# The last convolution's result moves to its own PSUM bank and runs half a tile later

## The reference

```python
x = x + _L0_conv_ref(_gn(x), ...)  # 25 overlapping patches an image, each convolved by the expert its gate picks
x = x + _L1_conv_ref(_gn(x), ...)  # 3x3 convolution, weights mixed per image by a sigmoid gate
x = x + _L2_conv_ref(_gn(x), ...)  # each pixel replaced by the nearest of 512 codebook vectors
x = x + _L3_conv_ref(_gn(x), ...)  # deformable 3x3: nine bilinear samples a pixel, then a 288 x 32 product
```

## Time and profile before

| | |
|---|---|
| median of 3 runs | 1956.34 us (1949.91 to 1961.21) |
| the profiled execution's own time | 1952.65 us |
| its span, first to last instruction | 1950.4 us |
| busy PE, DVE, POOL, ACT | 1593.0, 1442.8, 1208.6, 1102.4 us |
| mean granted TensorE clock | 0.926 of full speed |
| 280 us to 1786 us: fronts with halves between | seven periods of some 218 to 222 us |
| 1786 us to 1950 us: halves alone | PE busy 158.70 of 164.00 us |

### The profile page before, as it was taken

The page is one execution under the profiler, slowest core; times in us unless marked ns, Lnnn a source line. Parts: engine busy times, 40 slices in busy tenths (PEclk is TensorE's granted clock), DMA queues, the critical chain, the costliest instruction groups (busy, mean ns, idle before and its releaser), DMA issues.

```text
span 1950.4 us, 41631 instructions
## 1 busy us (share of the span) xinstructions
PE 1593.0 (82%) x15426; PEld 1302.8 (67%) x15426; DVE 1442.8 (74%) x2960; ACT 1102.4 (57%) x1499; POOL 1208.6 (62%) x1413
## 2 busy tenths in 40 slices
PE   0239557889988897989888898889988898989998
PEld 0112355669856786668866787658865797668998
DVE  3147546888779877888679778897779767896776
ACT  0001155558655676557655575657755585657986
POOL 4004245777657856677657756677657765677764
PEclk9955578999989999999999999999999998999999
DMA  7954695569846896569856796569856795235542
GB/s 145 212 116 119 148 214 169 150 179 228 219 125 188 206 219 182 150 172 234 219 148 188 185 220 195 151 172 239 220 155 179 188 228 154 76 87 155 150 148 79
DMA packets 294772, 336.84 MB, mean 173 GB/s; under 512 B 219600, under 2 KB 233936, under 8 KB 290348
## 3 DMA queue, kind: packets, MB, share of 16 engines
q1 hardware_dynamic: 240712, 228.88, 45.6%
q0 software_dynamic: 36336, 84.55, 17.8%
q10 hardware_dynamic: 17524, 20.75, 3.6%
HBM read 260.57 MB, written 60.09 MB: 164 GB/s over the span
## 4 chain that ended last, share of the span: by engine, by line
PE 46%; DVE 14%; DMA 11%; DVEq 7%; SPq 6%; issue 6%; ACT 4%; POOL 3%; ACTq 2%
PE bank L1307 25%; PE bank L1406 5%; DMA words<-in_codebook,code 5%; SPq L437 4%; PE bank L1294 4%; DVE code L1183 4%; DVEq L1182 3%; PE bank L1364 3%; PE bank L1391 3%; DVEq L976 3%; PE bank L1276 2%; PE bank L1291 2%; POOL words L622 2%; POOL fetched L599 2%; DVE samp L977 2%
## 5 line engine op out<-in xcount | busy, mean ns | idle before, releaser
L599 POOL DMA_INDIRECT fetched<-row_pairs,corner x768 | 738.8, 962 | 451.5 <-DVE weighted L971 248.7
L1307 PE MATMUL bank<-lent,tent 128*128 128x160 f32 x6144 | 955.3, 310 | 0.4 <-issue 0.4
L1307 PEld LDWEIGHTS bank<-lent,tent 128*128 128x128 f32 x6144 | 881.0, 196 | 95.9 <-issue 68.5
L733 ACT ACTIVATE tent<-lent,row_at_sb 128x768 f32<-128x768 f32 x512 | 449.2, 925 | 54.9 <-PE bank L1307 40.1
L963 DVE TENSOR_TENSOR strip<-bank,near 128x480 f32<-128x480 f32 x512 | 331.9, 651 | 186.0 <-PE bank L1307 181.0
L737 ACT ACTIVATE tent<-tent 128x1536 f32<-128x1536 f32 x256 | 380.0, 1484 | 21.0 <-issue 0.4
L622 POOL DMA_INDIRECT words<-in_codebook,code x256 | 244.0, 953 | 106.2 <-DVE code L1183 54.0
L977 DVE TENSOR_REDUCE samp<-strip 128x96 f32<-128x480 f32 x414 | 270.3, 653 | 39.6 <-issue 2.2
L1406 PE MATMUL bank<-cb,xs 64*128 64x512 f32 x512 | 245.8, 697 | 36.8 <-DVE code L1183 22.1
L819 ACT COPY xs<-xn 32x128 f32<-32x128 f32 x256 | 75.6, 295 | 259.9 <-PE bank L1406 242.5
L722 ACT COPY samp_t<-bank 96x384 f32<-96x384 f32 x256 | 119.9, 468 | 134.7 <-PE bank L1294 111.2
(11 more groups left out here) (136 smaller groups left out, 1113.1 us busy)
## 6 DMA issues: line engine op xcount, KB each, us to landing
lent<-z_rows SPq DMA_DIRECT2D x256, 384.0 KB
picked_weights<-arena SPq DMA_DIRECT2D x14, 1800.0 KB
arena<-picked_weights SPq DMA_DIRECT2D x21, 720.0 KB
arena<-windows SPq DMA_DIRECT2D x288, 50.0 KB
arena<-xp SPq DMA_DIRECT2D x96, 136.0 KB
fetched<-row_pairs,corner POOLq DMA_INDIRECT x768
arena<-row_pairs SPq DMA_DIRECT2D x64, 160.0 KB
slice<-picked_weights SPq DMA_DIRECT2D x14, 720.0 KB
```

Source lines behind the costliest of these rows:

```text
L599: pool.indirect_dma_start(fetched[:, N % FETCHES, k].rearrange("p q c -> p (q c)"), None, pairs_dram[b % 2], bass.IndirectOffsetOnAxis(ap= ...
L733: act.activation(w[:, piece], zs[:, N % SPREADS, :], ACT.Abs, bias=row_at[:, piece:piece + 1])
L1307: m = pe.matmul(STRIPS[j % 3][:, XW * C * e:XW * C * (e + 1)], tent[:, N % TENTS, c, DENSE * d + e], picture[:, b % 2, i, c], start=(c == ...
```

## The change

The result of the last convolution gets the first 128 columns of bank P2, in which nothing else lives any more. The wait of `turn_samples` for `copy_result` goes, and `convolve` waits for the `copy_result` before the last instead. `convolve` moves from half d = 1 of every fourth tile to half d = 0 of the tile after: it now stands in halves -12, -4, 4, 12, 20, 28, 36 and 44, after the strips and before `turn_samples`. `copy_result` moves from the start of half d = 0 to the half d = 1 after it, behind `copy_samples`. DVE's `add_x` and SP's `store` move one tile later. conv1 writes P0 and P1 in place of P1 and P2, and the cells P4 and P1 in place of P2 and P4. As the offsets still stand in P1, PE waits before the second set of cell transposes for the four DVE instructions that read them.

```diff
-        PO = PT[:, 384:512]
+        PO = P2[:, 0:128]
...
-        CELLS = [P2, P4]
+        CELLS = [P4, P1]
...
+        off_read = sem("off_read")
...
-                if n == 5 and b > 0:
+                if n == 6 and b > 0:
                     store(b - 1, 1)
-                if n == 21:
+                if n == 22:
                     store(b, 0)
...
-                if d == 0 and N % SET == 2 and N > SET:
-                    copy_result(N // SET - 1)
                 if d == 1 and N > 1:
                     copy_samples(N - 2)
+                if d == 1 and N % SET == 2 and N > SET:
+                    copy_result(N // SET - 1)
...
-                if n == 3 and d == 1 and b > 0:
+                if n == 4 and d == 1 and b > 0:
                     add_x(b - 1, 1)
-                if n == 19 and d == 1:
+                if n == 20 and d == 1:
                     add_x(b, 0)
...
-                    dve.tensor_tensor(x, x, PP[1 + h][:, :], ALU.add).then_inc(x2_ready, 1)
+                    dve.tensor_tensor(x, x, PP[h][:, :], ALU.add).then_inc(x2_ready, 1)
...
-                        dve.tensor_tensor(dst, src, at_grid.broadcast_to([128, IMG, ht, TAPS]), ALU.add)
+                        dve.tensor_tensor(dst, src, at_grid.broadcast_to([128, IMG, ht, TAPS]), ALU.add).then_inc(off_read, 1)
...
             def convolve(k):
                 pe.wait_ge(samp_sb, SET * (k + 1))
+                if k > 0:
+                    pe.wait_ge(result_sb, k)
...
-                if N >= SET:
-                    pe.wait_ge(result_sb, N // SET)
...
                 strips(N, d)
-                if d == 1 and N % SET == 1 and N > SET:
+                if d == 0 and N % SET == 2 and N > SET:
                     convolve(N // SET - 1)
...
-                            m = pe.matmul(PP[1 + h][C * i:C * (i + 1), :], mix[:, i, C * dx:C * (dx + 1)],
+                            m = pe.matmul(PP[h][C * i:C * (i + 1), :], mix[:, i, C * dx:C * (dx + 1)],
...
                     if f >= 2:
                         pe.wait_ge(cells_sb, FLATS * g + f - 1)
+                    if f == 1:
+                        pe.wait_ge(off_read, 4 * (g + 1))
```

## The result

The changed kernel takes 1940.71 us (median of 11 runs, 1931.53 to 1957.64), the kernel before 1956.34 in the same comparison. The ratio is 0.9917, 95% interval 0.9893 to 0.994: faster by 0.8%, some 16 us, where 42 were forecast. It lies above the range of 1893 to 1938. The profiled span is 1934.9 us after 1950.4.

What follows compares the result with a forecast made beforehand. PE was taken as busiest yet idle some 357 us, with 84.4 us of waits touched directly. Gains 25 + 12 + 7 - 0 - 2 = 42 us off 1952.65 gave 1910.7, with 3.7 added 1914; range 1893 to 1938.

Steps and rivals of the forecast that it cites:

- `pool`: Place where PE waited for ACT's result copy: DVE's wait for half 13's strips goes, 12 us gained, bounds 7 and 13.4.
- which clock?: Question at `norm2` whether PE runs at full or half clock after its wait: gain 4.0 or 2.0 us, 3.6 taken.
- `norm2`: Halves 19 to 20: strips move ahead of the waiting convolution, so scores start earlier; 25 us gained, bounds 14 and 28.
- `norm3`: Halves 43 to 44: offsets 3.0 us earlier on PE, but POOL is next; 7 us gained, bounds 0 and 17.
- The sentence on the Trainium skill: Throttled clock is the default, activity releases it; the convolution could be cold after any real wait, 11 us less.
- the remaining 2.4 us is below both: At `norm2`, PE's remaining idle was below waits of 2.69 and 2.79 us, so 3.6 us was taken, near the upper end.
- The sign that the prediction named: In half -12 of the first groups, PE's wait at L1291 grows to 2.5 us and more.
- The cells' wait: PE's new wait before the second cell transposes costs 0, covered by PE's lead; 4 us without that cover.
- The scores: Halves 28 and 36: PE's block before the next score is 1.0 us longer; 2 us lost, bounds 0 to 14.
- First group and end: What lies outside the measured stretches of groups one to seven: forecast 0.
- The "slower" rival: The later convolution delays scores in halves 20, 28 and 36, costing 25 us with the new wait: 1969 us, chance 0.04.
- the waits only move: Rival: ACT's copy stays behind the square root, PE waits one strip later; gain 19 us, 1937 us, chance 0.17.

Runs made afterwards that it cites:

- e2: Changed kernel with the convolution back in its old half everywhere, the result keeping its own bank: 1960.7 us, ratio 1.0038.
- e5: Changed kernel plus six matmuls of 128x448 that nobody reads, in PE's idle time before conv1: 1929.1 us, ratio 0.9845.
- e8: Changed kernel with four stacking DMAs for conv1 in place of twelve from the second group on, so stale rows: 1918.0 us, ratio 0.9815.
- e4: Changed kernel with the convolution in its old half everywhere except at `norm3`, where it stays late: 1950.5 us, ratio 0.9995.
- e1: Kernel before with only the change's new banks for conv1 and the cells, and PE's new wait: 1961.7 us, ratio 1.004.
- e11: Kernel before plus ten unread matmuls of 128x512 in PE's gap at `norm2`, order unchanged: 1990.5 us, ratio 1.0122.
- e13: Kernel before plus four unread matmuls of 128x512 in PE's gap at `norm2`, order unchanged: 1946.2 us, ratio 0.995.
- e3: Changed kernel with the convolution in its old half everywhere except at `norm2`, where it stays late: 1944.7 us, ratio 0.9929.
- e7: Changed kernel with the convolutions inside the scores (halves 27 and 35) back early, late everywhere else: 1936.3 us, ratio 0.9869.

## Why the prediction was wrong, and where it was right

**The step that failed** is one that the prediction didn't make. It moved conv1 forward by the whole of `pool`'s gain and kept its duration. It had seen the DMAs land at 982 to 983 and called that a possible loss of some microseconds in place; conv1 did start on their landing, at 981.66. It had also asked "which clock?" at `norm2`, and took gaps of 2.7 and 2.8 us as harmless, though one of the two rows has the strips behind at 3.56 us. It did not ask the same question at conv1, the one place where the change makes PE's gap longer. PE reaches it 3.8 us sooner in group four (978.42 after 982.20, the start of conv1 less the gap), but the DMAs let it go on only 3.0 us sooner; over the groups the gap went from 2.3 to 2.7 us to 2.3 to 3.7. The price was 17.9 us. e2 shows that it comes with the `pool` gain, e5 that it is clock, e8 that most of it goes with the DMAs. The trace of before held two warnings. conv1 had run slow in two of seven groups already, after 2.28 and 2.39 us. And the earlier trace rows are not typical: `norm3` has seven waits of 2.61 to 3.21 us, and behind six of them the strips took 3.1 to 3.6 us instead of 1.90.

```profile
539.87 5.34 PE L1391 MATMUL bank<-arena,mix 96*32 96x512 f32 x24 [2.28 <-DVE mix L1147]
...
1096.76 3.31 PE L1307 MATMUL bank<-lent,tent 128*128 128x160 f32 x12
...
1757.00 3.57 PE L1307 MATMUL bank<-lent,tent 128*128 128x160 f32 x12
```


The sentence on the Trainium skill (TensorE: Matmul & The Clock Gate, Part 1) in the prediction was weighed at `norm2` only and put aside on the earlier trace rows. conv1's 5.35 us after a wait agree with the rule as the page states it, throttled unless activity releases it; so do the 2.78 us behind the fillers. The 2.78 us after a wait of 3.17 show that it isn't every wait.

**Term by term.**
- *`norm2`, 25 us:* 20.1, or 25.5 to the first score less 5.4 because the scores then ran at half clock. The value lies inside the bounds of 14 and 28. The half clock came behind the convolution in six of seven groups, after gaps of 2.5 to 2.9 us. The sentence "the remaining 2.4 us is below both" was too sure.
- *`pool`, 12 us, bound 13.4:* 14.1. Right, and for the reason given on DVE's side: its seven waits for half 13 went. PE's side was wrong without harm: it stood for the samples' copy at once (2.73 us in group four), not first at 972.1.
- *`norm3`, 7 us:* the offsets came 3.2 us a group sooner (22.4), and 8.3 of it were lost again before the next addition, 6.0 of them behind the offsets: 14.1 net, in one trace. Some 3 us of these are the last group's and didn't last: it left its front 18 us ahead, and 15 us later, behind waits of 3.73 us on PE (the last row below) and 6.55 us on DVE, it was 15 ahead. Groups one to six alone gained 11.3 to the next addition: 6.6 in the first three, where the prediction had 0, and 4.7 in the others. e4, with nothing else late, was 10 us under e2 by the medians and 4 by the spans. The net sum was inside the bounds, and its reason half right. The sign that the prediction named, a longer wait of PE in half -12, is there: 14.8 us in seven groups after 7.9 (the first and the last below). But in the first three groups it is 1.80, 1.71 and 2.39 us, not 2.5 and more, so that part of the 3.2 us gets through, and the profile names DVE's sum in four of the seven, POOL's in one and none in two.

```profile
463.07 0.40 PE L1292 MATMUL bank<-ident_sb,samp 128*96 128x128 f32 x2 [1.80 <-DVE samp L978]
...
1764.20 0.64 PE L1292 MATMUL bank<-ident_sb,samp 128*96 128x128 f32 x2 [3.73 <-POOL samp L648]
```

- *The cells' wait, 0:* PE stood 4.2 us for it in eight groups, both after and in e1. Behind the offsets 6.0 us were lost after and 3.9 in e1, near the 4 us that the prediction named for a missing cover. It overlaps with what the rows give back, so its net cost stays open between 0 and 5 us.
- *The scores, 2 us:* +7.0 in the trace, but not due to this step as far as the runs show.
- *First group and end, 0:* +3.8. Some 1.3 us were lost before group one and are not explained; the rest is the last group's lead that the waits at the start of the last halves took back (see `norm3`).

The difference of 27 us is then 18 at conv1, 4 in front of it, 5 each at the first scores and in the scores, 4 at the ends, less 2 at `pool` and 7 at `norm3`. With the clock restored (and the cells' wait shortened) the same change stands at 1919.7, 6 us above the 1914 of the forecast. So the gains at `pool` and `norm2` came by the mechanism forecast, and at `norm3` the mechanism was half right. The "slower" rival had the wrong place and "the waits only move" the wrong one too, though its 1937 is the nearest of the times: it was reached by other losses than those that it named.

**Left open.** What exactly decides the clock: a first half was slow after gaps of 2.0 and 2.3 us and fast after one of 3.17. In the four kernels with the old wait at `pool` (before, e1, e11, e13) 12 of 28 first halves were slow, two to five of seven, and those stood behind the shorter gaps (2.23 to 2.46 us; the fast ones behind 2.49 to 3.11). With that wait gone and nothing else done for conv1 (after, e2, e3, e4, e7) it was 33 of 35. So the loss goes with the change at `pool`, and filling the gap removes it, but the longer gap and the sparser work in front of it were not told apart. A fix of conv1's DMAs that keeps the output (fewer rows copied, or issued earlier) wasn't tried.

## What to carry to other kernels

When a change moves an engine's work forward, ask for each wait that remains whether the gap in front of it grows, not only who ends it: TensorE can lose more in the clock of what follows than the wait grew (here some 0.7 us of gap and 2.57 us of conv1 in group four). Price the operation behind a longer gap at both durations, and count over all the trace of before how often it already shows the long one; two rows picked out of seven misled here. Matmuls into an unused bank can give the clock back: three at a place did at conv1 in five of seven groups, one didn't, and what exceeded the gap was lost in delay. And a gain that depends on a later stage should be followed to the next place where all engines meet, since `pool`'s 14 us by itself made nothing faster.

## What was not expected of the hardware

- A busy filler changes the speed of what follows: conv1's first half went from 5.3 to 2.7 us a group by adding 4.5 us of useless matmuls, and the kernel became 12 us faster (1940.7 to 1929.1).
- An FP32 matmul with 128 columns of weights and 448 or 512 of data took 0.75 and 0.86 us at full clock, shown as two records each.
- In all twelve traces in which PE's wait for the result's copy was gone, the stretch at `pool` gained 13.8 to 14.5 us. The scores and the rows, where POOL's indirect DMAs run, scattered by 10 us and more between variants that differ elsewhere. A term of a few microseconds can be read from one trace in the first kind of stretch, and not in the second.
